# Values of two heads made in one go from split products, with the value buffer doubled and the order of the step changed

## The reference, cut to what matters

```
k = concat(mem_k, xn @ Wk);  v = concat(mem_v, xn @ Wv)
dots = einsum(q, k) * scale, mixed over heads by pre_proj, causal mask
attn = softmax over the 8 largest of each row
attn = mixed over heads by post_proj
out  = einsum(attn, v) @ Wo + bo
```

## Time and profile before

| | |
|---|---|
| median of three runs | 1481.67 us |
| the profiled execution | span 1476.7 us from the first to the last instruction (the time around it is not in the profile) |
| busy | PE 1359.3 us (92%), PEld 1189.8, DVE 1117.9 (76%), ACT 800.0, POOL 857.3 |
| chain that ended last | PE 63%, DVE 15%, POOL 9%, "issue" 7%, ACT 3% |
| values (L1882 from n_all) | 1024 matmuls, 141.7 us busy, mean 281 ns of one |
| keys (L1882 from mt_all's parts) | 330 matmuls, 104.4 us busy |
| PE waited for POOL (L1864 <- L790) | 40.2 us in 56 waits |
| DVE waited for PE (L1381 <- L1855) | 151.8 us in 257 waits |

### The profile page before, as it was taken

How to read it: one execution, slowest core, us unless ns; L and a number is a source line. 1 busy time by engine, 2 the same in 40 slices (tenths; PEclk the granted TensorE clock), 3 DMA queues, 4 the chain that set the end, 5 groups by cost and what they waited for, 6 DMA issues and landing times.

```text
span 1476.7 us, 32500 instructions
## 1 busy us (share of the span) xinstructions
PE 1359.3 (92%) x10047; PEld 1189.8 (81%) x10047; DVE 1117.9 (76%) x3711; ACT 800.0 (54%) x1719; POOL 857.3 (58%) x1694
## 2 busy tenths in 40 slices
PE   5999998998899899999999999999999999899964
PEld 5558897886788789889888988988998889788842
DVE  7828785997788688788878878886887878554765
ACT  3646664444566566656666665665666566432321
POOL 5248783444776665745655574565557576633552
PEclk9999999999999999999999999999999999999997
DMA  7026002423300000000000000000000000012221
GB/s 250 12 82 210 25 23 86 121 73 99 98 19 3 18 16 9 18 12 9 9 14 16 8 17 11 10 7 16 16 9 10 19 11 5 12 51 76 64 82 41
DMA packets 70106, 62.25 MB, mean 42 GB/s; under 512 B 10808, under 2 KB 58019, under 8 KB 69938
## 3 DMA queue, kind: packets, MB, share of 16 engines
q1 hardware_dynamic: 61746, 44.96, 10.1%
q0 software_dynamic: 8192, 15.23, 3.5%
HBM read 32.88 MB, written 25.17 MB: 39 GB/s over the span
## 4 chain that ended last, share of the span: by engine, by line
PE 63%; DVE 15%; POOL 9%; issue 7%; ACT 3%; POOLq 2%; DVEq 1%; DMA 1%; SPq 0%
PE sa L1875 13%; PE sc L1853 11%; PE mb L1882 10%; PE tr L1864 7%; PE sc L1712 4%; DVE kept L1391 4%; POOL attn L790 3%; DVE top L1381 3%; PE mb L2091 2%; PE sc L1812 2%; PE sc L1855 2%; POOL x_slots L759 1%; PE sc L2079 1%; PE tr L1717 1%; PE sa L1919 1%
## 5 line engine op out<-in xcount | busy, mean ns | idle before, releaser
L790 POOL TENSOR_SCALAR attn<-kept,rden 128x128 f32<-128x128 f32 (+3 forms) x512 | 290.4, 567 | 340.3 <-DVE rden L1395 287.2
L1381 DVE MAX8 top<-sc 128x8 f32<-128x144 f32 (+3 forms) x512 | 263.2, 514 | 152.4 <-PE sc L1855 151.8
L1853 PE MATMUL sc<-k_hl,x_hl 128*128 128x272 f32 (+3 forms) x1920 | 370.0, 312 | 3.2 <-DVE k_hl L1373 1.7
L1875 PE MATMUL sa<-wv,attnT 128*128 128x128 f32 x2560 | 371.9, 276 | 0.0
L1021 ACT ACTIVATE attnT<-tr 128x128 f32<-128x128 f32 (+3 forms) x512 | 224.0, 437 | 269.2 <-PE tr L1864 257.5
L1875 PEld LDWEIGHTS sa<-wv,attnT 128*128 128x128 f32 x2560 | 327.7, 192 | 6.1 <-issue 6.1
L1015 ACT ACTIVATE ex<-sc,nmax 128x144 f32<-128x144 f32 (+3 forms) x512 | 277.5, 542 | 100.7 <-DVE nmax L1383 94.0
L1853 PEld LDWEIGHTS sc<-k_hl,x_hl 128*128 128x128 f32 x1920 | 280.9, 190 | 22.7 <-issue 12.4
L1391 DVE SCALAR_TENSOR_TENSOR kept<-sc,top,ex 128x144 f32<-128x144 f32 (+3 forms) x512 | 289.5, 565 | 0.6 <-issue 0.6
L1864 PE MATMUL tr<-ident,attn 128*128 128x128 f32 x1280 | 231.0, 279 | 42.4 <-POOL attn L790 40.2
L1864 PEld LDWEIGHTS tr<-ident,attn 128*128 128x128 f32 x1280 | 139.0, 142 | 56.0 <-POOL attn L790 51.6
(11 more groups left out here) (331 smaller groups left out, 1950.4 us busy)
## 6 DMA issues: line engine op xcount, KB each, us to landing
x_slots<-sg SPq DMA_DIRECT2D x1, 4608.0 KB, 17.0
y_slots<-wv SPq DMA_DIRECT2D x18, 256.0 KB, 2.3
x_slots<-sg SPq DMA_DIRECT2D x1, 2560.0 KB
y_pick<-x_slots SPq DMA_DIRECT2D x10, 256.0 KB, 2.8
fb<-L_ffn_b SPq DMA_DIRECT2D x2, 1024.0 KB, 9.6
attn<-x_slots SPq DMA_DIRECT2D x8, 256.0 KB, 3.4
arena<-L_attn_x SPq DMA_DIRECT2D x8, 256.0 KB, 3.1
fb<-L_ffn_W SPq DMA_DIRECT2D x8, 256.0 KB, 6.3
```

Source lines behind the costliest of these rows:

```text
L790: pool.tensor_scalar(dst, src[:, NM:NM + P * (t + 1)], rden[:, t:t + 1], 1.0, ALU.mult, ALU.mult).then_inc(attn_ready.sem, 1)
L1381: dve.max(top8[:, t, :], src).then_inc(top_done.sem, 1)
L1853: pe.matmul(dst[:, lo:hi], x_hl[:, a, t * P:(t + 1) * P], k_hl[:, m, k, lo:hi], start=(i == 0), stop=(i == 2 and hi < w), skip_group_check ...
L1875: ins = pe.matmul(sa[:, t * C:(t + 1) * C], src[:, j * P:(j + 1) * P], wv[:, j, k, :], start=False, stop=False, skip_group_check=True)
```

## The change

- `values(b, it, j)` now makes the values of both heads for half of the tokens (j = 0: blocks 0 and 1; j = 1: blocks 2 and 3). In sequences 1 to 7 it uses three partial products of 256 columns for each block (`x_hl` as weights, `n_hl`, the two parts of `n_all`, as moving operand): six fp32r products a call. In sequence 0 it uses two float32 products of 256 columns.
- `wv` has two buffers, used by turns of the pairs. `attend` waits for `values0` at block 0 and for `values1` at block 2 of the first head.
- The slots move: values to slots 2 and 4 (from 3 and 7), `keys0` of the next pair to slot 5 (from 4), its `keys_low` on DVE to slot 6 (from 5). `keys1` and its `keys_low` stay in slots 0 and 1.
- `split_n`, on POOL: in sequence 1 in slot 7 of each pair but the last (128x256), and once before it, writes `n_hl` into `w13_hl[:, 4:8]`. Since that space is taken till the end of sequence 7, `V1` is laid out anew, and its splits stand at six places; the last two come after the last `normalise` and wait for the last values.
- In sequence 1 ACT's first values wait for the stores of the first mixture, whose buffer is part of `wv`.

```diff
+        n_hl = w13_hl[:, 4:8, :, :].rearrange("p e w n -> p (e w n)").rearrange("p (a w n) -> p a w n", a=NIT, w=2)
         def v1_hl(e, w):
-            return w13_hl[:, (e + 4) % E1, w, :]
+            return w13_hl[:, e // 2 + 4 * (1 - e % 2), w, :]
-        wv = sb("wv", [P, NT, 2, C])
+        wv = sb("wv", [P, 2, NT, 2, C])
...
+            def split_n(it):
+                split([n_hl[:, it, w, :] for w in range(2)], n_all[:, it, :, :].rearrange("p k c -> p (k c)")).then_inc(n_split, 1)
...
-            V1_AT = ((0, 6), (1, 5), (2, 1), (2, 7), (3, 6), (4, 6), (6, 7), (7, 7))
+            V1_AT = ((2, 1), (2, 6), (4, 1), (4, 6), (6, 1), (6, 6))
...
+                        if b == 1 and it + 1 < NIT and u == 7:
+                            split_n(it + 1)
...
             normalise(B, 0, -1)
+            pool.wait_ge(*misc_done(B - 1, NIT - 1, "values1"))
+            for e in range(6, E1):
+                split_v1(e)
...
# ACT
-            def values(b, it, k):
-                act.wait_ge(av_done.sem, av_done.at(b, it * UNITS + (k - 1) * NT))
-                evacuate(b, it, f"values{k}", wv[:, :, k, :]).then_inc(misc_free.sem, 1)
+            def values(b, it, j):
+                if b or it > 1:
+                    act.wait_ge(av_done.sem, av_done.at(b, (it - 1) * UNITS))
+                if b == 1 and it == 0 and j == 0:
+                    for half in range(2):
+                        act.wait_ge(y0_stored[half], 16 * (GROUPS0 // 2))
+                evacuate(b, it, f"values{j}", wv[:, it % 2, 2 * j:2 * j + 2, :, :].rearrange("p t k c -> p (t k c)")
+                         ).then_inc(misc_free.sem, 1)
...
-                        if u == 3 or (u == 7 and it + 1 < NIT):
-                            values(b, it, int(u != 3))
+                        if u in (2, 4):
+                            values(b, it, int(u == 4))
...
-                        if u == 4 and it + 1 < NIT:
+                        if u == 5 and it + 1 < NIT:
                             keys(b, it + 1, 0)
...
# DVE
-                        if u == 5 and it + 1 < NIT:
+                        if u == 6 and it + 1 < NIT:
                             keys_low(b, it + 1, 0)
...
# PE
-                if t == 0:
-                    pe.wait_ge(*misc_left(b, u // UNITS, f"values{k}"))
+                if k == 0 and t in (0, 2):
+                    pe.wait_ge(*misc_left(b if u >= 0 else b - 1, u // UNITS % NIT, f"values{t // 2}"))
...
-            def values(b, it, k, guard):
-                return misc(b, it, f"values{k}", guard, [(t * C, C, xnT[:, t * P:(t + 1) * P], n_all[:, it, k, :], True, True)
-                                                         for t in range(NT)])
+            def values(b, it, j, guard):
+                if b == 0:
+                    both = n_all[:, it, :, :].rearrange("p k c -> p (k c)")
+                    return misc(b, it, f"values{j}", guard, [(i * 2 * C, 2 * C, xnT[:, (2 * j + i) * P:(2 * j + i + 1) * P], both,
+                                                              True, True) for i in range(2)])
+                if b == 1:
+                    pe.wait_ge(n_split, it + 1)
+                return misc(b, it, f"values{j}", guard,
+                            [(i * 2 * C, 2 * C, x_hl[:, m, (2 * j + i) * P:(2 * j + i + 1) * P], n_hl[:, it, w, :], n == 0, n == 2)
+                             for i in range(2) for n, (w, m) in enumerate(PARTS)])
...
-                        if u == 3:
-                            guard = values(b, it, 0, guard)
-                        if u == 7 and it + 1 < NIT:
-                            guard = values(b, it, 1, guard)
+                        if u in (2, 4):
+                            guard = values(b, it, int(u == 4), guard)
...
                         if u == 0:
                             guard = keys(b, it, 1, guard)
-                        if u == 4:
-                            guard = keys(b, it + 1, 0, guard) if it + 1 < NIT else values(b, it, 1, guard)
+                        if u == 5 and it + 1 < NIT:
+                            guard = keys(b, it + 1, 0, guard)
```

More of the change, by code:

```diff
@@ L208, in build @@
         y0_flat = y0_pick[:, :, :, :].rearrange("p k t c -> p (k t c)")
-        wv_flat = wv[:, :, :, :].rearrange("p t k c -> p (t k c)")
+        wv_flat = wv[:, 0, :, :, :].rearrange("p t k c -> p (t k c)")
         lg0 = wv_flat[:, 0:256].rearrange("p (b e) -> p b e", e=E0)
@@ L336, in build @@
         mt_split = sem("mt_split")
+        n_split = sem("n_split")
         cast_done = sem("cast_done")
@@ L444, in entry @@
         def entry(name, it):
[L446 to L452, removed]
+            return 4 * it + {"keys0": 1, "keys1": 2, "values0": 3, "values1": 4}[name]
         def misc_done(b, it, name):
@@ L829, in row @@
                                 pool.wait_ge(v_in, 16 * (2 * E1 + 1))
-                            if e >= 4:
-                                n = it * UNITS if it < NIT - 1 else it * UNITS + 5
-                                pool.wait_ge(sc_ready.sem, sc_ready.at(b, n))
+                            pool.wait_ge(*misc_done(b, 2 * (e // 2) + 1, "values1"))
                             split_v1(e)
@@ L878, in _ @@
             split_m(0, 1)
+            split_n(0)
             take_puts(0)
@@ L1079, in row @@
                             keys(b, it, 1)
-                        if u == 4 and it + 1 < NIT:
+                        if u == 5 and it + 1 < NIT:
                             keys(b, it + 1, 0)
-                        if u == 4 and it == NIT - 1:
-                            values(b, it, 1)
                         if it == NIT - 1 and u == 5 and not last:
@@ L1874, in attend @@
                 for j in range(t + 1):
-                    ins = pe.matmul(sa[:, t * C:(t + 1) * C], src[:, j * P:(j + 1) * P], wv[:, j, k, :],
+                    ins = pe.matmul(sa[:, t * C:(t + 1) * C], src[:, j * P:(j + 1) * P], wv[:, u // UNITS % 2, j, k, :],
                                     start=False, stop=False, skip_group_check=True)
```

## The result

The changed kernel takes 1510.91 us (median of four runs, 1506.12 to 1512.24), the kernel before, beside it on the same chip, 1480.66. The ratio is 1.0184, 95% interval 1.0159 to 1.0208: slower by 27 us by the ratio, by 30 between the two medians. I had forecast slower, by 13; the time lies above my range, whose end was 1508.

What follows compares the result with a forecast made beforehand. PE's list was taken to bound the kernel; -21 + 25.3 + 5.8 + 7 - 4 + 2.5 - 1.9 gave +13.7 us on the span, forecasting 1495 us, with an 8-in-10 range of 1475 to 1508.

Steps and rivals of the forecast that it cites:

- the clock: Rival: PE's added wait in pair 1 halves the clock for some 6 us a sequence; 1516 us, 0.12 including POOL.
- PE's waits for POOL: Transposes of slot 2 wait less behind `values0`, -4 us; splits of `n_all` in sequence 1 delay POOL, +2.5 us.
- What bounds the kernel: Sequences 1 to 7: PE's list sets the pace, so work taken off it shortens the time one for one.
- Values on PE: Sequences 1 to 7: six fp32r products take 0.75 us a call against 0.94, saving 21 us over 56 pairs.
- The new wait: Slot 2: `values0` waits for DVE's `keys_low` of slot 1, 25.3 us, growing by 7 in pairs 1 and 2.
- Weight loads in the open: Products starting after a wait on PE show their weight load: 54 waits by 0.107 us, +5.8 us.
- Splits on POOL in sequence 7: Six places for splits of `V1` in sequence 7 are the same sort as before: 0 us.
- The end: End of sequence 7: no split ahead of the last `normalise`, so PE's last transposes start 1.9 us earlier.
- Sequence 0: Values there use half the passes with twice the columns; gain of 0 to 1.5 us, taken as 0.

Runs made afterwards that it cites:

- e5: Changed kernel with values, keys and keys_low in the slots of the kernel before, six splits of `n_all` ahead of sequence 1; ratio 0.9948 to the kernel before.
- e1: Changed kernel with values0 issued in slot 3 instead of slot 2 on PE and ACT; 1496.06 us, ratio 1.0122 to the kernel before.
- e3: Changed kernel with DVE's pieces of the sequence before moved behind keys_low of slot 1 in sequences 2 to 7; ratio 1.0071 to the kernel before.
- e2: Changed kernel with plain fp32 products of 256 columns in all sequences and no `split_n`; 1511.04 us, ratio 1.0210 to the kernel before.
- e4: Changed kernel with all eight splits of `V1` behind the last `normalise`; ratio 1.0230 to the kernel before.
- e6: e5 with the six splits of `V1` in sequence 7 spread over other places; ratio 0.9961 to the kernel before.
- e7: e6 with plain fp32 products of 256 columns and no splits of `n_all`; ratio 0.9982 to the kernel before.

## Why the prediction was right and wrong

The direction and the main mechanism were right, the size was not: the span grew by 33.7 us, and my sum had 13.7. Two of its terms failed: the clock, which it had at nothing and which took some 12 us, and PE's waits for POOL, the splits of sequence 7 included, which it had at -1.5 and which grew by some 10. By its own steps, with waits counted as it counts them, from start to start on PE:

- **What bounds the kernel.** Right: DVE's step that frees `mb` was the place to look at. But "PE's list sets the pace" holds for one order only: in e5, 2.2 of some 2.9 us a sequence taken off PE's list came back; in e1, with the same work, 3.0 us a sequence were lost again to the order.
- **Values on PE, -21.** Right. From a mask product to the row behind the call it is 1.01 us before and 0.83 after where nothing is waited for, 0.18 less; 112 calls give 20. The products cost what I took (117 to 119 ns from one to the next); the first takes 0.20 us, not 0.15, but the call starts 0.03 us sooner. In e5 slot 3 falls from 2.31 to 2.13 us and slot 7 to 2.11.
- **The new wait, +25.3, grown by 7.** Right in sum: 33.7 us over the 64 pairs, against 32.3. (The page's 24.3 in 25 waits leave out what lies under the 0.23 us of the mask product.) The make-up was not quite as read: 24 waits of over 0.5 us make 28.7, with 2.02 in pair 1 and 1.10 in pair 2 of sequences 2 to 7, against 1.44 and 0.85 as read and some 0.5 more as grown; 18 of 0.2 to 0.4 us make 4.6, where 36 had been read, and 22 pairs have none. In pair 3 of sequence 4 PE waits 0.2 us for POOL in slot 1 and so comes late enough for DVE. e3 shows that the long ones come from DVE's list.
- **Weight loads in the open, +5.8.** Not seen. The first product of `values` takes 0.22 us behind a wait and 0.20 without one. The 504 ns of the earlier trace rows are of a product with no idle time ahead of it (at 438.63 us).
- **PE's waits for POOL, -4 and +2.5.** By the page they grew by 2.7 us, from start to start by some 10: 4.4 in sequence 7, 3.4 in sequence 1, under 1 in each of the others. In sequence 1 the page has 13.3 us against 10.7 before; e2, without the splits of `n_all`, has 10.0. The fall that I hoped for elsewhere did not come (a fourth of 40.2 us, halved, would have been 5.0, not 4).
- **Splits on POOL in sequence 7, "0".** This step failed. Sequence 7 grew by 11.1 us, 8.3 more than sequences 2 to 6, and without the splits it takes no more than they do (e4). It is not the places alone: in e5 the same six places make sequence 7 longer than the others by 5.7 us, in e6 six other places by 5.5; before, eight splits did so by 2.5. In the changed kernel three drops of the clock come with them, some 5 us at the 1.6 of pair 1.
- **The clock, a rival with 0.12 together with POOL.** This step failed most. I took it to be all or nothing, weighed it by a wait of 1.10 us that had left the clock alone, and put nothing of it into the sum. It came in part: eight drops in the sequences, where before had none. Four in pair 1 cost 1.6 us each, the one at the start of sequence 0 1.2; with 1.6 for the three in sequence 7, an estimate, that is some 12 us. The mean granted clock is 0.981 against 0.988. The Trainium skill ("TensorE: Matmul & The Clock Gate", "Part 1: The HAM clock gate") says that the hardware's activity window runs freely, so that one kernel can show different amounts of slow clock; the equal waits of sequences 2 to 7, four with a drop and two without, agree with that, and so do the four runs of the changed kernel, with mean clocks from 0.981 to 0.986. I should have priced the waits of 1.4 us and more with a share of drops.
- **The end, -1.9.** It gave 3.2. PE's last transposes start 4.1 us behind the last mask product (1315.50 to 1319.56), where I had 3.7; that is 1.6 of it, and the rest I have not separated.
- **Sequence 0.** I gave it only waits of 0.2 us. It lost 4.8 us without a split in it. e4, with the same list there and no drop, takes 121.0, so 1.2 are the clock. The other 3.6 are order, since e7, with the same products in the places of before, takes 117.0: in most pairs PE stands for 0.2 us ahead of the transposes of slot 1 and for 0.2 to 0.3 ahead of the values of slot 2. The page does not show these as waits, and PE's busy time grew instead, from 116.1 to 120.8 us.

Together -20 + 34 + 10 + 12 - 3 and 1.5 in front of sequence 0 come to 34 or 35, against 33.7. What decides whether the clock falls behind a given wait stays open: 1.83 us did it four times of six, 1.77 in e2 never; behind the splits of sequence 7 waits of 1.96, 1.74 and 1.78 us did it each time, and 1.94, 1.74 and 1.91 in e1 not once.

## What to carry to other kernels

When a step is moved to an earlier place in an engine's list, look up what the engine that frees its buffer does first in its own list there: the pieces of other work ahead of that step cost more than the new products saved, and moving them behind it cost nothing. The same work taken off the bound engine gave 2.2 us a sequence in one order and lost 0.8 in another (e5, e1), so ask of each place what the other engines have to do there. Count a short wait from start to start: the page's idle time leaves out what lies under a product in flight, here up to 0.19 us each. Before work is put into an engine's gap, find out from a second kernel whether the gap stays where it is when the work ahead of it changes.

## What the runs showed of the hardware

- In the changed kernel the granted clock fell to 0.50 for some 3 us behind seven of nine waits of 1.74 to 1.96 us between stretches in which PE was full; in e1 it fell behind none of three such waits. Where the same pair ran with and without a drop, the drop cost 1.6 us more than the wait itself.
- From the start of one row to the next, a pass of a plain float32 product takes 216 ns with 256 columns and 112 with 128; an fp32r product of 256 columns takes 118. So the wider plain product saves little: 0.98 us from the mask product to the row behind the call in e7, 1.01 before, 0.83 with split products (sequences 2 to 6 of e7: 124.7 us against 125.4 before, with the double buffer in).
- POOL stood for 5.55 us at the start of the code of sequence 1 in all eleven kernels, whether it came there at 358 or at 368 us; what it is, no run here tells.
